# Expert products by slot: rows scattered to their expert's slots through device memory, multiplied once, and gathered back

## The reference

```python
y1 = _ln(x + _mha(...), ln1_g, ln1_b)
def _moe(x, wg, w1, b1, w2, b2):                  # S = 2048 tokens, E = 8 experts
    cap = int(CAP_FACTOR * S) // E                # 256 slots an expert
    gates = jax.nn.softmax(xf @ wg, axis=-1)
    idx = jnp.argmax(gates, axis=-1)
    mask1 = jax.nn.one_hot(idx, E, dtype=x.dtype)
    loc = jnp.sum((jnp.cumsum(mask1, 0) - 1.0) * mask1, -1).astype(jnp.int32)
    keep = loc < cap
    gate_val = jnp.take_along_axis(gates, idx[:, None], -1)[:, 0]
    slot = jnp.where(keep, idx.astype(jnp.int32) * cap + loc, E * cap)
    disp = jnp.zeros((E * cap, D), x.dtype).at[slot].set(xf, mode='drop')
    h = jnp.einsum('ecd,edf->ecf', disp, w1) + b1[:, None, :]
    y = (jnp.einsum('ecf,efd->ecd', h, w2) + b2[:, None, :]).reshape(E * cap, D)
    return jnp.where(keep[:, None], gate_val[:, None] * y[jnp.minimum(slot, E * cap - 1)], 0.0)
y2 = _ln(y1 + _moe(y1, wg, w1, b1, w2, b2), ln2_g, ln2_b)
return x_of_the_layer + y2
```

## Time and profile before

| | |
|---|---|
| median of 3 runs | 1749.46 us (1747.46 to 1750.39) |
| profiled execution | 1742.33 us |
| its span | 1740.6 us |
| granted TensorE clock, mean | 0.96 |
| busy over the span | PE 1593.1 us (92%), DVE 1133.3 (65%), ACT 435.5 (25%), POOL 428.7 (25%) |
| data moved | 145.48 MB |

### The profile page before, as it was taken

How to read it: one execution, slowest core, us unless ns; L and a number is a source line. 1 busy time by engine, 2 the same in 40 slices (tenths; PEclk the granted TensorE clock), 3 DMA queues, 4 the chain that set the end, 5 groups by cost and what they waited for, 6 DMA issues and landing times. The chain is left out here.

```text
span 1740.6 us, 27161 instructions
## 1 busy us (share of the span) xinstructions
PE 1593.1 (92%) x10778; PEld 949.2 (55%) x10778; DVE 1133.3 (65%) x3320; ACT 435.5 (25%) x671; POOL 428.7 (25%) x357
## 2 busy tenths in 40 slices
PE   7988889999999986989898878999999997988998
PEld 3446678888888873433343333444445583447443
DVE  1549798777696461687886656438834984146776
ACT  2332111020202001323232332211124783133100
POOL 0003314150415223357576655000000000013000
PEclk9999899999999997999899989999999998998999
DMA  8900000000000124656576755200510270000000
GB/s 356 212 6 2 2 1 9 2 9 2 9 8 3 33 91 127 247 159 187 158 229 191 236 154 162 109 0 5 189 61 18 79 230 0 7 1 1 13 13 25
DMA packets 79105, 145.48 MB, mean 84 GB/s; under 512 B 41354, under 2 KB 49666, under 8 KB 76418
## 3 DMA queue, kind: packets, MB, share of 16 engines
q1 hardware_dynamic: 58498, 76.61, 13.4%
q0 software_dynamic: 20480, 67.13, 12.9%
HBM read 137.42 MB, written 10.49 MB: 85 GB/s over the span
## 5 line engine op out<-in xcount | busy, mean ns | idle before, releaser
L514 PE MATMUL peer_ps_h<-all_x,layer_down 128*128 128x256 f32 x768 | 179.7, 388 | 0.0
L650 POOL TENSOR_TENSOR peer_bm<-peer_bm,peer_slots 128x512 f32<-128x512 f32 x36 | 109.1, 3030 | 245.3 <-DVE peer_bm L746 245.3
L1420 PE MATMUL skills_acc<-skills_hid,skills_w 128*128 128x512 f32 x256 | 130.6, 636 | 35.5 <-DVE skills_hid L1153 31.6
L514 PEld LDWEIGHTS peer_ps_h<-all_x,layer_down 128*128 128x128 f32 x768 | 144.1, 192 | 21.5 <-issue 1.9
L553 PE MATMUL peer_ps_o<-peer_hg,layer_up 128*128 128x256 f32 x640 | 142.3, 380 | 0.5 <-DVE peer_hg L778 0.5
L553 PEld LDWEIGHTS peer_ps_o<-peer_hg,layer_up 128*128 128x128 f32 x640 | 120.5, 190 | 20.5 <-issue 3.3
L595 ACT ACTIVATE peer_hg<-peer_ps_h 128x512 f32<-128x512 f32 x96 | 57.3, 597 | 274.5 <-PE peer_ps_h L514 274.5
L1473 PE MATMUL skills_ps_g<-all_x,skills_w 128*128 128x512 f32 x256 | 122.0, 599 | 0.0
L1473 PE MATMUL skills_ps_u<-all_x,skills_w 128*128 128x512 f32 x256 | 120.3, 592 | 0.0
L1420 PEld LDWEIGHTS skills_acc<-skills_hid,skills_w 128*128 128x128 f32 x256 | 50.5, 201 | 102.9 <-issue 61.4
L1487 ACT ACTIVATE skills_act_g<-skills_ps_g 128x512 f32<-128x512 f32 x96 | 56.3, 597 | 193.8 <-PE skills_ps_g L1473 168.0
(11 more groups left out here) (413 smaller groups left out, 2735.9 us busy)
## 6 DMA issues: line engine op xcount, KB each, us to landing
four_ring<-in_l_w SPq DMA_DIRECT2D x8, 1024.0 KB, 4.9
quant_w<-in_l_w SPq DMA_DIRECT2D x32, 256.0 KB, 4.6
all_early<-in_l_w SPq DMA_DIRECT2D x26, 256.0 KB, 3.6
four_skill<-in_skills SPq DMA_DIRECT2D x2, 3072.0 KB
skills_w<-in_skills SPq DMA_DIRECT2D x2, 3072.0 KB, 11.0
layer_down<-in_down SPq DMA_DIRECT2D x1, 4096.0 KB, 25.6
layer_up<-in_up SPq DMA_DIRECT2D x1, 4096.0 KB, 35.3
expert_rows<-in_up SPq DMA_DIRECT2D x1, 4096.0 KB, 41.2
```

Of the source, the lines that this page charges most:

```text
L514: mm = pe.matmul(ps_h[group % 2][:, r, :], down[:, c, j * P:(j + 1) * P], g.x[:, c, bass.ds(i * PB, PB)], start=(c == 0), stop=(c == C - 1))
L650: pool.tensor_tensor(bm[c % RING][:], bm[c % RING][:], slots[half][:, 2, c * PAIRS:(c + 1) * PAIRS].unsqueeze(2).to_broadcast([P, PAIRS, WJ]),
L1420: mm = pe.matmul(acc[q % 2][c][:], w_down[s][:, m, c * P:(c + 1) * P], hid[j % 4][:], start=(s == 0 and m == 0), stop=(s == 2 and m == M2 ...
```

## The change

It is confined to `tail`, and two device-memory tensors: `slot_rows` (4096 rows of D) and `out_rows` (2049 rows). In words:

- `count` computes, for each token, its slot: expert x 256 + place, or T + token number when it is over capacity. The second part of `slot_rows` only takes those.
- POOL first makes two index tables (iota) and clears `held`, 16 x 256 elements a partition; SP writes these zeros over the 2048 slots and the one row T of `out_rows`.
- POOL scatters the rows of `y1t` to `slot_rows`, one indirect DMA a tile (128 rows of 1 KB), each pair as soon as its slots are known.
- When all 16 have landed, SP loads the slots back to `held` in four DMAs of 512 KB. For each expert TensorE transposes its two tiles, ScalarE copies them, TensorE multiplies them by that expert's matrix alone, VectorE adds the offset row, SP stores 256 KB to `out_rows`.
- When all eight stores have landed, POOL gathers `out_rows` back, one indirect DMA a tile, by `row` = min(slot, T).
- Per pair VectorE adds `weight` x row to `y1t`, takes statistics of both tiles; ScalarE now applies the second normalisation; the rest is as before, per pair.

The core of the diff:

```diff
         def count(p):
                 then(dve.tensor_tensor(keep[:, of, :], ps_c[p % 2][:, 0, :, :], before[:, of, :], ALU.add))
-                s.did(dve.scalar_tensor_tensor(out=hot[:, of, :], in0=keep[:, of, :], scalar=float(CAP), in1=hot[:, of, :],
-                                               op0=ALU.is_le, op1=ALU.mult))
                 marks["counted", p] = s.n
+                then(dve.scalar_tensor_tensor(out=hot[:, of, :], in0=keep[:, of, :], scalar=float(CAP), in1=hot[:, of, :],
+                                              op0=ALU.is_le, op1=ALU.mult),
+                     dve.tensor_tensor(spot[:, of, :], keep[:, of, :], spot0[:, of, :], ALU.add))
+                then(dve.tensor_tensor(spot[:, of, :], spot[:, of, :], hot[:, of, :], ALU.mult))
+                then(dve.tensor_reduce(slot_f[:, of], spot[:, of, :], AX_X, ALU.add))
+                then(dve.tensor_tensor(slot_f[:, of], slot_f[:, of], own[:, of], ALU.add))
+                s.did(dve.tensor_copy(slot[:, of], slot_f[:, of]))
+                marks["slot", p] = s.n
...
+            def outputs(e):
+                dve.wait_ge(n_ready, NPAIR + e + 1)
+                dve.wait_ge(spread_done, 2 + e // 2)
+                dve.tensor_tensor(z[:, 2 * e:2 * e + 2, :], ps_n[e % 2][:], c_rows[:, e, :].unsqueeze(1).to_broadcast([P, 2, D]),
+                                  ALU.add).then_inc(n_done, 1)
+
+            def mix(p):
+                dve.wait_ge(g.row_load[p % NRING], landed(p))
+                if p >= 2:
+                    dve.wait_ge(n2_done, p - 1)
...
+                    s.did(dve.scalar_tensor_tensor(out=acc[p % 2][:, i, :], in0=held[:, t, :], scalar=weight[:, t:t + 1],
+                                                   in1=y1t[:, t, :], op0=ALU.mult, op1=ALU.add))
...
+            for e in range(E3):
+                outputs(e)
+            for p in range(NPAIR):
+                mix(p)
+                if p > 0:
+                    give(p - 1)
+                spread2(p)
             give(NPAIR - 1)
...
+            for i in range(NPAIR + 4):
...
+                if i == 4:
+                    pool.wait_ge(rows_written, 16 * 2)
+                if i >= 4:
+                    p = i - 4
+                    pool.wait_ge(vstep, marks["slot", p])
+                    pool.wait_ge(y1t_step, 2 * (p + 1))
+                    for t in range(2 * p, 2 * p + 2):
+                        pool.indirect_dma_start(g.slot_rows, bass.IndirectOffsetOnAxis(ap=slot[:, t:t + 1], axis=0),
+                                                y1t[:, t, :], None).then_inc(g.row_load[0], 16)
+            pool.wait_ge(g.row_load[0], scattered)
+            pool.wait_ge(vstep, marks["row"])
+            pool.wait_ge(rows_written, 16 * (2 + E3))
+            for p in range(NPAIR):
+                if p >= NRING:
+                    pool.wait_ge(g.row_load[p % NRING], landed(p - NRING))
+                for t in range(2 * p, 2 * p + 2):
+                    pool.indirect_dma_start(held[:, t, :], None, g.out_rows, bass.IndirectOffsetOnAxis(ap=row[:, t:t + 1], axis=0)
+                                            ).then_inc(g.row_load[p % NRING], 16)
...
-            def expert(t, j):
...
-                    mm = pe.matmul(bank[n % 4][:], y1f[:, c, tokens(t)], g.w12[:, c, 2 * j:2 * j + 2, :], start=(c == 0), stop=(c == C - 1))
+            def turn_slots(e):
+                pe.wait_ge(slot_load[2 * e // per], 16)
+                pe.wait_ge(y1f_done, NPAIR * C + max(e - 1, 0))
...
+            def expert(e):
+                pe.wait_ge(y1f_done, NPAIR * C + e + 1)
...
+                        mm = pe.matmul(ps_n[e % 2][:, i, :], turned[e % 2][:, c, i * P:(i + 1) * P], g.w12[:, c, e, :],
+                                       start=(c == 0), stop=(c == C - 1))
...
+            sp.wait_ge(presets, 6)
+            sp.dma_start(at_slots, held[:]).then_inc(rows_written, 16)
+            sp.dma_start(g.out_rows[T:T + 1, :], held[0:1, 0, :]).then_inc(rows_written, 16)
+            sp.wait_ge(rows_written, 16 * 2)
+            sp.wait_ge(g.row_load[0], scattered)
+            for i in range(len(slot_load)):
+                sp.dma_start(held[:, i * per:(i + 1) * per, :], at_slots[:, i * per:(i + 1) * per, :]).then_inc(slot_load[i], 16)
+            for e in range(E3):
+                sp.wait_ge(n_done, NPAIR + e + 1)
+                sp.dma_start(at_out[:, 2 * e:2 * e + 2, :], z[:, 2 * e:2 * e + 2, :]).then_inc(rows_written, 16)
```

261 lines of the change are left out of this document (134 added, 127 removed).

## The result

The changed kernel takes **1690.86 us** (median of 4 runs, 1689.77 to 1693.33); the kernel before, run beside it, 1748.46 (4 runs, 1747.16 to 1750.39). The ratio is 0.9676, 95% interval 0.9658 to 0.9695: 57.6 us or 3.2% faster. Forecast were 1695.0, 1680 to 1715, faster with 0.96.

What follows compares the result with a forecast made beforehand. The prediction took TensorE's 136.6 us of all-expert products as the bound; the next chain (routing, memory passages, experts, finish) gives back some 82, so 54.3 us less than 1749.46 gives 1695 us, range 1680 to 1715.

Steps and rivals of the forecast that it cites:

- What bounds the kernel before: Expert part of the last stage: its 136.6 us are TensorE's, from products of every token with all eight experts.
- Routing: Slot counting on VectorE: 2.0 us more in each of four pairs beside POOL arithmetic, then 2.5 for the last four.
- POOL and SP cost nothing: During routing: POOL's library load (5.8 us) and clearing (3.7), and SP's writing of zeros (12.6), stay off the path.
- Scatter and load: After the last slot: wake-up, two scatters and landing take 4.6 us, loading the first slots back 3.6.
- Experts: Eight experts at 2.18 us of TensorE each, 17.4, plus first copy 1.0 and clock climb 2.1: 20.5 us.
- the climb: Start of the experts: TensorE's clock rising from its lower level costs 2.1 us, bounds 0 and 17.4.
- the first copy: Start of the experts: ScalarE's first copy of transposed slots is not hidden and adds 1.0 us.
- rival of a clock that stays low: TensorE's clock stays at the lower level through the experts: 15.3 us more, 1710; chance 0.12.
- The way back: From last expert product to rows gathered: offset add, wake-up and store 3.6 us, then two gathers and landing 4.6.
- The finish: Last per-pair work, paced by VectorE: eight rounds of 3.6 us, 28.8, bounds 3.3 and 4.0 a round.
- The wait for the transposes: In each finish round, VectorE waits 0.1 to 0.3 us for the transposes of the pair before.
- The sum and the time: Whole kernel: span ends at 1686.3 instead of 1740.6, 54.3 us less; the median 7 us above the profiled execution gives 1695.

Runs made afterwards that it cites:

- e5: Kernel before the change, with VectorE adding only the second of each two expert outcomes, all products kept; ratio to the unedited kernel before 0.9994.
- e6: Kernel before the change, with expert products of 256 columns, one expert of each two, and all adds kept; ratio 0.9895, last stage 166.7 us.
- e2: Changed kernel with POOL's multiply and add of pairs 4 to 6 held until the slot of four pairs before is written; ratio 0.9640, last stage 129.4 us.
- e10: Changed kernel with the output stores of all pairs but the last left out, scatters and gathers kept; one run, last stage 132.3 us.
- e11: Changed kernel with 32 tiny unused VectorE memsets added behind the reciprocal of the weights; one run, ratio 0.966, last stage 134.2 us.
- e9: Changed kernel with the edits of e2 and e3 and two 512-wide products behind the offset rows, before the experts; ratio 0.9625, last stage 125.3 us.
- e12: e9 plus outcomes written in place over x and output stores begun only after all gathers have landed; ratio 0.9610, last stage 123.1 us.
- e4: Changed kernel with six extra 512-wide TensorE products ahead of, between and behind the offset rows, outcome unread; ratio 0.9687, last stage 138.7 us.
- e8: Changed kernel without the stores of z and the gathers, the mix reading z in its own place; ratio 0.9644, last stage 123.7 us.
- e3: Changed kernel whose finish gives the pair two back instead of one back behind each mix; ratio 0.9677, last stage 133.7 us.
- e1: Changed kernel unedited, run again as base for the other runs; 1698.8 us, ratio 0.9686, last stage 135.0 us.

## Why the prediction was right

Each step against the trace of after, in us from the stage's first instruction (that of before is at 1552.71, so the prediction's 1614.5 is 61.8):

| step | predicted | measured |
|---|---|---|
| last slot | 61.8 | 62.4 |
| first slots turned | 70.0 | 70.3 |
| first gather issued | 94.1 | 94.6 |
| first mix | 98.7 | 98.7 |
| last mix round done | 127.5 | 127.5 |
| last give done | 130.6 | 130.7 |
| end | 133.6 | 133.7 |

- **What bounds the kernel before.** Right, and shown by e5 (half the adds, nothing gained) and e6 (half the products, 21 us): TensorE.
- **Routing.** The 2.0 a pair for the pairs with POOL beside them is what the rounds show (7.94 and 7.78 for 5.84). The mechanism, a count instruction that waits for the end of POOL's second operation, is shown by e2. Two stand-stills of 0.34 and 0.76 in VectorE's last count are of the kind told under e10; they cost nothing, as the step on the scatters shows.
- **POOL and SP cost nothing.** Nearly: the library load took 6.8 for the 5.8 of the earlier trace rows, and VectorE waited 0.40 once for `y1t`. The first scatter did not wait for the zeros.
- **Scatter and load.** 8.2 predicted, 7.9 measured, but one step of it is another than I thought. POOL's last ten scatters follow each other with 0.3 between, 1.28 each, and that is just VectorE's pace in the last four pairs (2.56 a pair), so POOL decides when the last one ends: 64.9 us into the stage in after, 65.0 in e11, whose last slot was written 0.9 earlier. From there to the first turned slot it is 5.4 in both (predicted 5.9: 2.3 and 3.6).
- **Experts.** 20.5 predicted from first turn to last product, 20.7 measured; the climb was 1.1 + 1.9 + 0.4 = 3.4 over the full-speed 0.87, 1.89 and 0.60, for 2.1 expected, and the period 2.17 for 2.18. Against that the first copy, for which I had 1.0, was hidden behind the transposes of the second expert, so the sum of this step came out right by two errors against each other. The climb is not a fixed price either: the same step took 19.8 to 21.4 to the last `z` in traces whose TensorE list is the same. The rival of a clock that stays low fell, as the clock was up after the first expert. That it starts low was right, and e9 and e12 show that products just ahead of the experts have them start high. The Trainium skill (TensorE: Matmul & The Clock Gate, Part 1) has the lower level as the default that activity lifts; the traces agree that products just ahead lift it, but in e4 the level was lost again in offset rows.
- **The way back.** 3.6 from the last product to the issue of the gather, which holds the last offset add; measured 3.7, of it 2.95 behind the add. 4.6 for the gather, measured 4.03, a little high. e8 gives the price of the passage, 7.0.
- **The finish.** Rounds of 3.6 expected, 3.48 measured, and one of 5.2 with VectorE's stand-stills (0.60, 0.71 and 0.92), which nothing in the prediction foresaw and whose cause stays open. So the sum of 28.8 is right by luck: without them it would be 27.1 or so. The wait for the transposes was 0.47 a round where I had 0.1 to 0.3. That VectorE waits for rows only in the first round held for the change as it stands, but no longer once its rounds were shortened (e9, e12).
- **The sum and the time.** The span was foreseen to 0.1 (after the 1.66 of a later start), closer than its steps deserve: the experts and the finish each came right by errors that cancel. The median was 4 lower than forecast for another reason: I had added 7 us, the distance of the profiled execution of before from its median. In after that distance is 1.1. It belongs to an execution, not to a kernel: VectorE's stand-stills in the earlier stages vary by more than that from one to the next.

## What to carry to other kernels

Before work is taken off the fullest engine, write the next chain out in full and price the change by it: 136.6 us of TensorE went, 82 came back, and halving the products alone would have brought 21. A passage through device memory by index and back cost 7 to 8 us each way here, and both engines' starts behind it are worth a look: with two cheap products placed in the wait the expert step was 0.6 to 2.4 us shorter than in the traces without them, while with six, some of them ahead of it, the stage was 3.7 us longer in its trace. When VectorE handles two SBUF inputs beside POOL arithmetic, order POOL behind it if POOL has the time: 5.6 us for two lines.

## What I had not expected of the hardware

- TensorE's clock stayed at 0.50 through 7.2 us of uninterrupted products with 8 rows (3.78 and 3.62 a group of four), and in e4 fell from 1.00 to 0.50 between two groups of them, while products of 128 rows lay between. In the finish, where four transposes in 1.12 us run every 3.5 us, it is 0.50 throughout.
- VectorE can stand still between two instructions of its own with nothing shown that it waits for, up to 9.7 us in an earlier stage (e3) and 3.08 in this one, more often in some groups of executions than in others. Part of the 70 us between the groups lies there: at one line 52.0 us of such waits in e1 and 22.2 in e11, and TensorE's waits there 37.1 and 1.8. A change of a few microseconds can't be read from whole times across groups.
- Gathers of the same size cost the DMA engines four times as much in their second half, and stores beside them land in 7.8 us instead of 2.6. The likely cause, one row read by nearly all descriptors, was not tried.
